# Gate logits with the weights held, and 128 weight columns in products that hold tokens

## What is computed

```python
gates = softmax(xn @ gate_W + gate_b)              # 1250 x 4, top 2 of 4 experts are used
for e in range(4):                                  # experts, two layers each
    h = relu(aggr(xn) @ Wl[e,0] + bl[e,0] + xn @ Wr[e,0])
    h = relu(aggr(h) @ Wl[e,1] + bl[e,1] + h @ Wr[e,1])   # computed as aggr(h @ Wl)
for i in range(2):                                  # mixer
    q, k, v = y @ Wq[i] + bq, y @ Wk[i] + bk, y @ Wv[i] + bv
    scores = q_or_k_of_a_head @ proj[i].T           # 256 features a head
    x = x + o @ Wo[i] + bo
    x = x + gelu(y @ W1[i] + b1) @ W2[i] + b2
```

## Time and profile before

| | |
|---|---|
| median of 3 runs | 2229.84 us |
| lowest, highest run | 2223.46, 2231.34 us |
| the profiled execution | 2227.69 us |
| its span, first to last instruction | 2225.9 us |
| mean granted TensorE clock | 0.931 |

### The profile page before, as it was taken

How to read it: one execution, slowest core, us unless ns; L and a number is a source line. 1 busy time by engine, 2 the same in 40 slices (tenths; PEclk the granted TensorE clock), 3 DMA queues, 4 the chain that set the end, 5 groups by cost and what they waited for, 6 DMA issues and landing times. The chain is left out here.

```text
span 2225.9 us, 28867 instructions
## 1 busy us (share of the span) xinstructions
PE 1960.4 (88%) x9764; PEld 1607.9 (72%) x9765; DVE 891.4 (40%) x1745; ACT 607.0 (27%) x1113; POOL 592.4 (27%) x408
## 2 busy tenths in 40 slices
PE   0767998999999989998989989999799898899992
PEld 0444656888888867776979977788688798778881
DVE  8777612111111134444134446422532353462237
ACT  5722102111111111104234552112142364331110
POOL 3000213232323123206312003433262300063332
PEclk9999898999999999998787899999888798999996
DMA  2010402121311285226621100111164111001111
GB/s 52 1 48 0 153 0 81 72 104 71 104 71 66 94 284 165 95 86 164 169 73 40 46 20 1 39 38 39 55 166 131 47 43 62 1 29 48 39 47 46
DMA packets 75221, 160.62 MB, mean 72 GB/s; under 512 B 9616, under 2 KB 24500, under 8 KB 73306
## 3 DMA queue, kind: packets, MB, share of 16 engines
q1 hardware_dynamic: 75092, 158.92, 22.3%
HBM read 103.30 MB, written 55.59 MB: 71 GB/s over the span
## 5 line engine op out<-in xcount | busy, mean ns | idle before, releaser
L561 PE MATMUL ps<-yT,wslot 128*128 128x500 f32 (+1 forms) x576 | 210.3, 365 | 13.4 <-POOL wslot L1706 4.8
L563 PE MATMUL ps<-yT,wslot 128*128 128x500 f32 (+1 forms) x576 | 206.8, 359 | 0.0
L562 PE MATMUL ps<-yT,wslot 128*128 128x500 f32 (+1 forms) x576 | 206.8, 359 | 0.0
L787 PE MATMUL ps<-g,adj 125*125 125x512 f32 x800 | 191.3, 402 | 16.9 <-issue 16.9
L787 PEld LDWEIGHTS ps<-g,adj 125*125 125x125 f32 x800 | 151.4, 190 | 56.8 <-issue 18.2
L1706 POOL TENSOR_TENSOR wslot<-mix_landing,wslot 128x2048 fp32r<-128x2048 f32 x24 | 110.9, 4622 | 213.3 <-ACT wslot L1389 213.3
L1710 POOL TENSOR_TENSOR hidT<-qpT,hidT 128x500 fp32r<-128x500 f32 (+1 forms) x96 | 104.4, 1090 | 197.9 <-DVE hidT L1544 197.9
L358 PE MATMUL ps<-key_hot,row_hot 125*125 125x500 bf16 x430 | 106.4, 388 | 46.0 <-DVE key_hot L328 35.8
L561 PE MATMUL ps<-parts,w 128*128 128x500 f32 (+1 forms) x384 | 136.4, 355 | 6.2 <-DVE bl L904 6.2
L1440 ACT ACTIVATE qpT<-ps,layer_cols 128x500 f32<-128x500 f32 (+1 forms) x96 | 58.2, 609 | 287.7 <-PE ps L563 243.0
L562 PE MATMUL ps<-parts,w 128*128 128x500 f32 (+1 forms) x384 | 136.3, 355 | 0.0
(11 more groups left out here) (262 smaller groups left out, 3822.4 us busy)
## 6 DMA issues: line engine op xcount, KB each, us to landing
mix_landing<-in_L_mix_W SPq DMA_DIRECT2D x16, 1024.0 KB, 5.1
qk_dram<-qk_parts SPq DMA_DIRECT2D x128, 125.0 KB, 2.4
g_dram<-staged SPq DMA_DIRECT2D x40, 256.0 KB, 2.0
u_dram<-staged SPq DMA_DIRECT2D x40, 256.0 KB, 2.0
g_in<-g_dram SPq DMA_DIRECT2D x40, 256.0 KB, 3.6
u_in<-u_dram SPq DMA_DIRECT2D x40, 256.0 KB, 2.7
k_stack<-qk_dram SPq DMA_DIRECT2D x8, 1250.0 KB, 6.2
q_stack<-qk_dram SPq DMA_DIRECT2D x8, 1250.0 KB, 8.2
```

The lines of the kernel that those rows point to most:

```text
L561: nc.tensor.matmul(out, lhs_high, rhs_high, start=first, stop=False)
L562: nc.tensor.matmul(out, lhs_high, rhs_low, start=False, stop=False)
L563: return nc.tensor.matmul(out, lhs_low, rhs_high, start=False, stop=last)
L787: last = nc.tensor.matmul(m.ps[0:P, t % 2, :], counts if exact else counts.bitcast(F32), part if exact else part.bitcast(F32), start=(s == ...
```

## The change

The gate logits are computed the other way round: the four columns of gate_W are held and xnT streams in the three chunks, into banks 0 to 2 of PSUM, four rows each. ScalarE, after its first two copies of xnT, copies these rows to gate_rows (the first rows of inv_row, which is written only later), and TensorE turns them with ten transpositions into bank 3, where VectorE reads them as before. The transpositions stand ahead of the second sum (n == 1); the degree products stand ahead of the third (n == 2) instead of the second. VectorE waits for gate_summed to reach 2.

Products that hold a tile of tokens hold 128 columns, the tile and the first three tokens of the next one, and write 128 rows of PSUM, of which 125 are read as before. The last tile of a group keeps 125. One semaphore of the start, ident_cleared, becomes part of consts_made, whose waits rise from 7 to 8.

```diff
@@ tile
+def wide(t, last=T - 1):
+    return slice(t * P, t * P + (P if t == last else 128))
+
+
+def out_rows(t, last=T - 1):
+    return slice(0, P if t == last else 128)
@@ stage_index_and_count, gpsimd
-                pool.memset(m.ident[:], 0.0).then_inc(ident_cleared, 1)
-                pool.wait_ge(ident_cleared, 1)
+                pool.memset(m.ident[:], 0.0).then_inc(consts_made, 1)
+                pool.wait_ge(consts_made, 1)
...
-                act.wait_ge(consts_made, 7)
+                act.wait_ge(consts_made, 8)
...
@@ stage_gates_and_first_sum
+        gate_rows = inv_row[0:EXPERTS]
...
@@ tensor
                 pe.wait_ge(gate_loaded, 32)
-                for t in range(T):
+                for i, (c0, cn) in enumerate(CHUNKS):
                     for k in range(K):
-                        last = nc.tensor.matmul(m.ps[0:P, 3, GATES_AT + t * EXPERTS:GATES_AT + (t + 1) * EXPERTS], m.xnT[:, k, tile(t)], gw[:, k, :],
-                                                start=(k == 0), stop=(k == K - 1))
+                        last = nc.tensor.matmul(m.ps[0:EXPERTS, i, 0:cn], gw[:, k, :], m.xnT[:, k, c0:c0 + cn], start=(k == 0), stop=(k == K - 1))
                 last.then_inc(gate_summed, 1)
                 n = 0
                 for f in range(K):
                     for c0, cn in CHUNKS:
                         if n == 1:
+                            pe.wait_ge(gate_rows_ready, len(CHUNKS))
+                            for t in range(T):
+                                last = nc.tensor.transpose(m.ps[0:P, 3, GATES_AT + t * EXPERTS:GATES_AT + (t + 1) * EXPERTS], gate_rows[:, tile(t)],
+                                                           m.ident[0:EXPERTS, 0:EXPERTS])
+                            last.then_inc(gate_summed, 1)
+                        if n == 2:
 
                             pe.wait_ge(deg_part_ready, 1)
                             pe.wait_ge(gate_shifted, 1)
@@ scalar
-                for k in range(K):
+                for k in range(2):
+                    nc.scalar.activation(m.parts[:, XN, 0, k, :], m.xnT[:, k, :], ACT.Copy).then_inc(xn_high, 1)
+                act.wait_ge(gate_summed, 1)
+                for i, (c0, cn) in enumerate(CHUNKS):
+                    nc.scalar.activation(gate_rows[:, c0:c0 + cn], m.ps[0:EXPERTS, i, 0:cn], ACT.Copy).then_inc(gate_rows_ready, 1)
+                for k in range(2, K):
                     nc.scalar.activation(m.parts[:, XN, 0, k, :], m.xnT[:, k, :], ACT.Copy).then_inc(xn_high, 1)
@@ vector
-                vec.wait_ge(gate_summed, 1)
+                vec.wait_ge(gate_summed, 2)
@@ stage_experts, second_layer
-                                last = emit_split_product(nc, m.ps[0:P, 4 + t % 2 * 2 + wt, :],
-                                                          [hT[:, c % 2, h, k, at:at + P] for h in range(2)],
+                                last = emit_split_product(nc, m.ps[out_rows(t, TILES[c][-1]), 4 + t % 2 * 2 + wt, :],
+                                                          [hT[:, c % 2, h, k, at:at + (P if t == TILES[c][-1] else 128)] for h in range(2)],
@@ counts_times_g
-                            counts = adj[:, t // 2, s, tile(t % 2)]
+                            at = s * SPAN + t % 2 * P
+                            counts = adj[:, t // 2].rearrange("p s d -> p (s d)")[:, at:min(at + 128, T * SPAN)]
...
-                                last = nc.tensor.matmul(m.ps[0:P, t % 2, :], counts if exact else counts.bitcast(F32),
+                                last = nc.tensor.matmul(m.ps[0:counts.shape[1], t % 2, :], counts if exact else counts.bitcast(F32),
@@ stage_mixer: scores, V, Wo, W2
-                            last = nc.tensor.matmul(m.ps[0:P, bank, h * M:(h + 1) * M], stack[:, h, tile(t)], projT[:, part, :],
+                            last = nc.tensor.matmul(m.ps[out_rows(t), bank, h * M:(h + 1) * M], stack[:, h, wide(t)], projT[:, part, :],
...
-                            last = emit_split_product(nc, m.ps[0:P, t % 2, :], [yT[:, h, k, tile(t)] for h in range(2)],
+                            last = emit_split_product(nc, m.ps[out_rows(t), t % 2, :], [yT[:, h, k, wide(t)] for h in range(2)],
...
-                                last = emit_split_product(nc, m.ps[0:P, 6 + t % 2, :], [yT[:, h, k, tile(t)] for h in range(2)],
+                                last = emit_split_product(nc, m.ps[out_rows(t), 6 + t % 2, :], [yT[:, h, k, wide(t)] for h in range(2)],
...
-                                    last = emit_split_product(nc, m.ps[0:P, t % 2, :], [hT[:, h, k, tile(t)] for h in range(2)],
+                                    last = emit_split_product(nc, m.ps[out_rows(t, t1 - 1), t % 2, :], [hT[:, h, k, wide(t, t1 - 1)] for h in range(2)],
```

## The result

The changed kernel takes 2211.82 us (median of 9 runs, 2208.36 to 2220.81) and the kernel before, on the same chip, 2227.22 us (9 runs, 2222.39 to 2231.34).

The account below looks back on a forecast made before the run. TensorE, its matmuls busy 88% of the span, was taken as the bound. Gate-stage terms of -6.2 - 2.1 + 1.1 + 1.7 = -5.5 us and 0 for 128 columns gave 2224.3 us, range 2214 to 2235.

Parts of the forecast that it names:

- Gates: Gate logits: 24 passes instead of 80, taking 10.5 us instead of 16.7, 6.2 us saved.
- first sum: Sum right behind the gate logits: begins at the higher clock, 8.4 us instead of 10.5, 2.1 us saved.
- transpositions: Ten added behind the first sum, 0.105 us each: 1.1 us, up to 1.6.
- halt: New TensorE wait for VectorE's mean ahead of the fifth sum, as degree products move later: 1.7 us.
- the stage: Gate stage in total: -6.2 - 2.1 + 1.1 + 1.7 = -5.5 us.
- (A): The forecast itself: long passes lift the clock in the gate stage, 128 columns are free; 2224.3 us, chance 0.74.
- (B): Rival: clock stays low in the gate stage, so the kernel is slower, +2.8 us, 2232.6 us; chance 0.12.
- (C): Rival: longer weight loads show, 4 ns on each of 3112 wide products; +6.9 us, 2236.7 us; chance 0.07.
- (D): Rival: full 128-column width makes each of 3112 products 11 ns faster; about 2190 us; chance 0.07.
- The range: Whole kernel's time: 2214 to 2235 us.
- the forecast's own line for "faster": Whole kernel: below 2218.7 us counts as faster, about 0.5% (11 us) being distinguishable from no change; chance 0.14.
- It carries through: End of the sums: the 5.5 us saved reach the result, since the experts begin behind a barrier after the last sum.

Follow-up runs that it names:

- The run with the place restored: Gate part alone (products keep 125 columns) plus 23 small fp32 matmuls ahead of it, against the kernel before: 2222.05 us against 2227.97, ratio 0.9975.
- +144: Kernel before with 36 small matmuls (144 instructions more) ahead of the loop over the counts: 2219.74 us against 2227.15, ratio 0.9966.

## Why the forecast was wrong

**Right, term by term.** Gates 10.5 forecast and 10.2 measured, first sum 8.4 and 8.6, transpositions 1.1 and 1.2, halt 1.7 and 1.55, the stage -5.5 and -5.3; the end of the sums carries through to the experts' first product. The clock rises in the gates, as in (A), so (B) falls. 128 columns are worth 0 within 4 us in a run of their own, so (C), (D) fall. The run with the place restored leaves 5.6 us, within an interval that holds these terms.

**In part luck.** That the stage came out within 0.2 us is owed to the pair of profiles. Seven kernels with the old gates take 117.9 to 120.5 us up to the experts' first product (mean 119.6), and the one profiled before is the fastest of them: in the others the clock stood at 1.2 GHz again for some 3.4 us around 258 to 263 us. Eight kernels with the new gates, the degree products where the change puts them, take 110.9 to 113.5 us (mean 112.6). So the gate part is worth 7.0 us by the means. The range was missed partly by its base: the forecast subtracts from 2229.84 us, the median of three runs, and the median of nine is 2227.22, which alone moves 2.6 us. By the forecast's own line for "faster", 2218.7 us, the kernel is faster, to which it gave 0.14, half of it for (D), which did not come true.

**The step that failed** is the zero behind "It carries through": the stage's end does carry through, but the sum has no term for what the missing instructions do to the loop over the counts, which it leaves at 0. It took for granted that passes added or removed cost only their own time, and that what comes after in the program runs as it ran. They also shift every later TensorE instruction inside the 16 KB pieces in which they are fetched, and by its place this kernel's loop fetches in its second turn or doesn't. The counts stage gave 7.8 us that no term of the sum had (9.5 by the means of all profiles); moving the place without any gain in the gates gives 0.0034 x 2227 = 7.6 us. Together 5.6 + 7.6 = 13.2 us, against 0.0067 x 2227 = 14.9 us for the change (15.4 by the medians); the interval of each of the three, some 4 us or more either way, is wider than what lies between them. By the means of the stages, 7.0 + 9.5 = 16.5 us, the sum comes out as far on the other side.

**The missing rival** was to be had from the profile before. "L787 <- issue" with 16.9 us in three waits was one of TensorE's largest waits, and none of the views asked what lay behind it. The forecast even used one of the same kind of halt, 846 to 853 us with TensorE busy for 4.59 of 7.00 us, but only as evidence on the clock. The branches there lasted 3.6 to 5.7 us each, and the instruction queue moved 11 packets from 885 to 990 us. A rival "the loop is fetched anew in each turn, and 92 instructions fewer change what is fetched" would have had a price from those rows: a halt of 4.79 us and the slow stretch after it. Its direction would have stayed open, as the pattern of places shows. So a range that reached some 8 us further down was the fair one.

**What the place does, as far as shown.** The Trainium skill, "Advanced Engine Details and Errata", section "ISA Cache", gives 16 KB for a line of the instruction cache and 128 KB in all for TensorE. The traces agree with the first, by packets of 16 KB and by +144 giving the short branches that stand on both sides of -112. By the two figures eight pieces would fit, which is an estimate. That the second turn fetched 9 to 11 packets where it fetched any, and none where it fetched none, fits a loop that needs one piece too many and so loses all of them. This is argued: no run shows which pieces stay. "Only 2 cache lines!", which stands in the same section of the Trainium skill beside 32 KB for the other engines, doesn't hold for this loop, whose executed half alone is 400 products or 800 instructions a turn, more than three pieces by the estimate of 64 bytes, and comes round without a packet in the changed kernel. The Trainium skill, "Advanced Engine Details and Errata", section "Control Flow Timing", gives about 0.1 us for a compare-and-branch; the traces have 0.2 us for a taken one where no packet was fetched, and 3.3 to 6.5 us where packets were.

**Open.** The exact place between 80 and 92 instructions less at which it tips, and the other one between 120 and 164 less; that one piece too many evicts all; that places repeat every 256 instructions, beyond the one pair -112 and +144. The profiled executions differ by up to 14 us behind the counts stage (1220 to 1234 us, with a mean granted clock of 0.91 and 0.89), so their totals don't settle a few us: the profiled one of the run with the place restored had a span of 2213.8 us, though its median is 2222.05. The stages were compared instead, and medians for totals.

## What to carry to other kernels

A change in the number of instructions ahead of a loop can move the loop's own time, in either direction, though nothing in it is touched. So, where a loop with far branches lies behind an edit, read the taken branches' durations and the instruction queue's packets in a second turn before costing the edit, and put that time into the range. When a gain comes from a stage that the edit doesn't touch, repeat the edit with its instructions made up by idle ones: that run separates the work saved from the place, as long as the idle ones leave the clock as it was. A far If inside a loop is worth trying ahead of it: here the traces show 4 us less up to the end of the loop, which the times don't tell from nothing.

## What was not expected of the hardware

- Far branches of TensorE took 3.3 to 6.5 us each where packets of instructions were fetched and 0.2 us where none were. Some of it hides under the products still queued: three second-turn branches of 3.4, 5.3 and 3.6 us show as one halt of 4.79 us.
- The clock pays too: behind that halt it was granted at 1.2 GHz for about 7 us (898.6 to 905.4).
- 144 instructions of useless work made the kernel 7.4 us faster (interval 0.2 to 15 us), and the stage that they touched by place alone went from 198.1 to 190.8 us.
- Over passes with four weight columns and 500 moving ones the clock went from 1.2 to 2.4 GHz 4.7 us after their start; over 16.7 us of passes with 125 weight columns and four moving it stayed at 1.2 GHz, both with TensorE busy throughout.
